# Turning eight tiles back by transposes before the first FFN, with theta begun in the last head

## The chip, the cores and the metric

One core of a Trainium2 chip. The metric is device time in microseconds: 641.4 us, the median of three runs of the kernel before (641.22 to 642.78).

## The reference, cut to what matters

x and ctx are (8, 256, 512), float32.

```python
x = x + tanh(g_xattn[0]) * L0_xattn(ctx, ctx, layernorm(x), ssm_kernel, D, 8)   # 32 heads of 8 channels: causal convolution
x = x + tanh(g_ffn[0])   * L0_ffn(layernorm(x), w1, b1, w2, b2)                 # int8 linear, exact gelu, int8 linear
x = x + tanh(g_xattn[1]) * L1_xattn(layernorm(x), ctx, theta_w, theta_b, ...)   # theta = theta_w @ ctx + theta_b, softmax, ...
x = x + tanh(g_ffn[1])   * L1_ffn(x, ...)                                       # 1.58-bit FFN
```

Both linears of the first FFN quantise their input with one scale for the whole tensor, so no product of the FFN can begin before the largest absolute value of all of layernorm(x) is known. theta needs ctx and weights alone.

## The kernel before, in words

The 2048 rows of x are 16 tiles of 128 x 512, taken in the order `order1` (even tiles first; numbers n below are places in it) in four groups of G = 4. Everything is ordered by hand: each engine has one instruction stream, and streams meet at semaphores `S[...]`.

**Heads.** In L0's attention each of the 32 heads runs through all engines: ScalarE repeats channels (`repeat_q` L830, `repeat_c` L809), GpSimd forms the pairs (`pairs` L612), TensorE multiplies by the Toeplitz matrix (`head` L1190, 20 passes of 128x288, banks 0 to 3 or 4 to 7 in turn), VectorE multiplies by q and sums (`head` L1622, the last instruction is L1638), GpSimd adds halves (`add_halves` L622) into `qT`. For the last head VectorE itself does the halves (L1693, L1695; semaphore `o_done`). Banks of PSUM have free columns beyond 288, in which other transposes travel with a head.

**Beside the heads.** Heads 20 to 27 turn back the tiles n = 0 to 7 by four transposes each (L1204), and VectorE adds them, read backwards and times tanh(g), to x (`back_add`, L1666). ScalarE turns the weights of the last FFN into ternary values (`ternary` L869, L873), whose loads and stores are SyncE's; in the loop of ScalarE, iteration h does `repeat_q(h + 1)`, `repeat_c(h + 2)`, then two `ternary` (in h = 28 the numbers 20 and 21, in h = 29 22 and 23). VectorE widens w1 from int16 to bf16 (`w1_widen` L1614) after heads 28 to 30, GpSimd the last quarter (L655).

**From head 31 to the first FFN.** TensorE adds x itself by a product with the identity (L1264) for six tiles, then turns tiles n = 8 to 15 back by products with `gated`, a reversed identity times tanh(g) (L1276). ScalarE copies six of them out of PSUM (L920), VectorE adds two (L1704). VectorE takes the maxima (`largest` L1677, L1679) and the statistics (L1557, L1561), GpSimd the scales (`norm_scales` L583), ScalarE normalises (L770). Then the maximum over all (transposed by TensorE, L1293), the scale `isx` (L1720), ScalarE's quantisation (`quant_x`, L945, two of them with `theta_out` between), VectorE's widening (`xqb_ready`, L1746), and TensorE's first linear (`mm1` L1308, L1313) with ScalarE's gelus (L952). The weights of theta and b1 are transposed after head 31 (L1260, L1262) and copied out by ScalarE (L926) and VectorE (L1697); eight `theta(b)` (L1286, four passes each, on the context loaded early by SyncE, L421 and L423) stand between those products, and `theta_out` (L932) takes each out.

**The store of x.** Group 0 of the hidden layer overwrites x, so x goes to HBM: GpSimd adds b2 to ten tiles after `xqb_ready` 3 (L661 to L663) and to six more (L666), SyncE stores each group when it is ready (`x1_save` L433, L437), and ScalarE's third group of gelus waits for all four (L969). In SyncE's queue the DMA transposes of the quantised tiles (L446) stand between these stores.

```python
            pool.wait_ge(S["xqb_ready"], 3)                                    # L661
            for t in order1[:10]:
                pool.tensor_tensor(x_res[:, t, :], x_res[:, t, :], b2b[:, :], ALU.add).then_inc(S["xb_added"], 1)

            gelu(1, 3, range(FT))
            act.wait_ge(S["x1_saved"], 16 * NG)                                # L969
            gelu(2, 0, range(FT))
```

## Time and profile before

| | |
|---|---|
| median of the runs | 641.4 us |
| the profiled execution | 643.1 us |
| its span | 641.3 us |
| mean granted clock of TensorE | 0.997 |
| busy: TensorE, VectorE, ScalarE, GpSimd | 95%, 85%, 74%, 55% of the span |
| chain that ended last | TensorE 65%, VectorE 12%, ScalarE 7% |
| the heads end (last head's product) | 196.4 us from the span's start |
| first product of the first FFN | 221.9 us |
| last product of its first linear | 283.4 us |

The profile is of one execution. A shares' table says which engine is worked hardest; what a change in one stretch is worth is read from the chain of waits in that stretch. Times in the rows are from the span's start.

### The profile page before, as it was taken

Reading aid. Unit: us, or ns where it says so; the run is one execution under the profiler, and the core shown is the slowest. Engines: PE = TensorE matmul, PEld = TensorE weight load, DVE = VectorE, ACT = ScalarE, POOL = GpSimd, SP = SyncE. Lnnn points to the kernel's source line nnn. Section 1 sums busy time; section 2 is a strip of 40 time slices with the busy share of each in tenths; the row PEclk is TensorE's granted clock in tenths of the full one; section 3 lists DMA queues with packets and bytes.
Section 4 is the critical chain, followed back from the end, with each engine's and each line's share of the span. In section 5 each row is a group of like instructions: output and inputs, shape, how many; then the busy total and the mean of one; then the engine's idle time right before and its main releaser. Section 6 shows DMA issues by size and latency. Waiting matters only on the chain.

```text
span 641.3 us, 9316 instructions
## 1 busy us (share of the span) xinstructions
PE 609.0 (95%) x2769; PEld 358.2 (56%) x2798; DVE 546.6 (85%) x1066; ACT 473.8 (74%) x718; POOL 351.9 (55%) x430
## 2 busy tenths in 40 slices
PE   5899999999999998989999999999888999999997
PEld 5777777777776443444445556555433444444443
DVE  2697888889999789976779988889898999999964
ACT  4469785765655896888672477766689999999984
POOL 1579888888874292310001111114487989898861
PEclk9999999999999999899999999999999999999999
DMA  8959896799999389838549920000116666656651
GB/s 300 377 192 310 291 327 223 260 323 339 332 299 331 134 285 311 223 94 327 198 98 167 255 56 16 16 17 17 50 33 162 185 177 183 164 180 164 182 162 50
DMA packets 141973, 125.20 MB, mean 195 GB/s; under 512 B 96032, under 2 KB 103984, under 8 KB 140784
## 3 DMA queue, kind: packets, MB, share of 16 engines
q1 hardware_dynamic: 134496, 110.52, 56.8%
q10 hardware_dynamic: 7440, 14.24, 6.6%
...
## 4 chain that ended last, share of the span: by engine, by line
PE 65%; DVE 12%; ACT 7%; issue 6%; DMA 4%; POOL 3%; SPq 2%; ACTq 0%; POOLq 0%; DVEq 0%
PE ps L1195 22%; PE ps L1475 14%; PE ps L1491 8%; PE ps L1313 4%; PE ps L1402 3%; PE ps L1432 3%; PE ps L1344 3%; DMA arena<-in_x 2%; ACT turn L989 2%; POOL arena L663 2%; PE ps L1450 2%; PE ps L1406 2%; SPq L446 2%; PE ps L1204 2%; DMA x_d<-arena 1%
## 5 line engine op out<-in xcount | busy, mean ns | idle before, releaser
L1195 PE MATMUL ps<-arena 128*128 128x288 f32 x640 | 160.6, 407 | 1.6 <-DVE inv_s L1661 0.9
L1195 PEld LDWEIGHTS ps<-arena 128*128 128x128 f32 x640 | 119.4, 190 | 33.5 <-DVE inv_s L1661 0.9
L1475 PE MATMUL ps<-arena 128*128 128x512 bf16 x510 | 113.5, 379 | 4.5 <-DVE arena L2066 4.3
L1475 PEld LDWEIGHTS ps<-arena 128*128 128x128 bf16 x512 | 49.4, 98 | 66.9 <-DVE arena L2066 5.7
L721 POOL TENSOR_TENSOR arena<-arena 128x512 f32<-128x512 f32 x64 | 80.4, 1276 | 8.6 <-DVE arena L2066 7.7
L618 POOL TENSOR_TENSOR arena<-arena 128x1024 f32<-128x1024 f32 x32 | 60.6, 1894 | 19.9 <-issue 12.3
L1313 PE MATMUL ps<-arena 128*128 128x512 bf16 (+1 forms) x249 | 57.1, 387 | 3.7 <-ACT arena L952 3.2
L1491 PE MATMUL ps<-arena 128*128 128x512 bf16 x241 | 57.1, 379 | 1.9 <-ACT arena L1103 0.7
L1344 PE MATMUL ps<-arena 128*128 128x512 bf16 x251 | 55.3, 379 | 1.2 <-DVE arena L1815 0.9
L952 ACT ACTIVATE arena<-ps,b,s 128x512 f32<-128x512 f32 x64 | 48.5, 778 | 10.6 <-DMA x_d<-arena 5.3
L625 POOL TENSOR_TENSOR turn<-turn 128x512 f32<-128x512 f32 x31 | 40.5, 1307 | 20.8 <-DVE turn L1638 20.8
L2066 DVE SCALAR_TENSOR_TENSOR arena<-ps,up_scale,arena 128x512 f32<-128x512 f32 x64 | 46.7, 745 | 5.8 <-ACT arena L1079 4.8
L579 POOL TENSOR_TENSOR ve<-mv,eps_ln 128x2 f32<-128x2 f32 x8 | 1.6, 198 | 87.5 <-DVE mv L1850 87.5
L1628 DVE TENSOR_TENSOR turn<-ps,arena 128x768 f32<-128x768 f32 x32 | 30.6, 955 | 18.3 <-PE ps L1204 15.5
L1313 PEld LDWEIGHTS ps<-arena 128*128 128x128 bf16 x256 | 25.3, 99 | 35.3 <-ACT arena L952 4.3
L1079 ACT ACTIVATE arena<-ps,up_scale 128x512 f32<-128x512 f32 x64 | 42.1, 675 | 3.9 <-PE ps L1475 3.8
L2073 DVE TENSOR_REDUCE q<-arena 128x1 f32<-128x1024 f32 x32 | 38.7, 1213 | 4.2 <-POOL arena L721 4.2
L1344 PEld LDWEIGHTS ps<-arena 128*128 128x128 bf16 x256 | 25.0, 98 | 30.8 <-issue 1.1
L1491 PEld LDWEIGHTS ps<-arena 128*128 128x128 bf16 x256 | 24.7, 98 | 30.7 <-ACT arena L1103 0.8
L715 POOL TENSOR_TENSOR arena<-turn,arena 128x1024 f32<-128x1024 f32 x16 | 37.8, 2363 | 5.5 <-ACT turn L1074 5.2
L1638 DVE TENSOR_TENSOR turn<-ps,turn 128x1024 f32<-128x1024 f32 x32 | 39.2, 1225 | 1.1
L873 ACT ACTIVATE late<-arena,inv_s 128x1024 int16<-128x1024 f32 x24 | 27.1, 1142 | 17.1 <-DMA arena<-in_L_ffn_w 15.5
...
## 6 DMA issues: line engine op xcount, KB each, us to landing
...
arena<-in_ctx SPq DMA_DIRECT2D x2, 2048.0 KB, 10.3
```

Of the source, the lines that this page charges most:

```text
L618: pool.tensor_tensor(dst[:, :, 0:32].rearrange("p r (d i) -> p r d i", d=4), a, shifted, ALU.mult)
L625: po.done(pool.tensor_tensor(x[:, :, 0:16], x[:, :, 0:16], x[:, :, 16:32], ALU.add))
L721: pool.tensor_tensor(hg[:, s, sl], hh[:, s, sl], g3[:, sl], ALU.mult).then_inc(S["hg_done"], 1)
L952: act.activation(hid[:, q, f, :], ps[:, f % 4, :], ACT.Gelu, bias=b1[:, f:f + 1], scale=s1[:, f:f + 1]).then_inc(S["gelu_done"], 1)
L1079: act.activation(sil[:, c, :], ps[:, up_banks(t, c)[0], :], ACT.Silu, scale=up_scale[:, s, 0:1]).then_inc(S["sil_done"], 1)
L1195: last = pe.matmul(ps[:, 4 * s + lo, 0:NB * PAIRS], toep[:, u, (LB - 1 - lo + li) * P:(LB - lo + li) * P], kv[:, s, li, :], start=(li == 0 ...
L1313: last = pe.matmul(ps[:, f % 4, :], fw1T[:, k, f * P:(f + 1) * P], xqT[:, k, ds(L * r, L)], start=(k == 0), stop=(k == LB - 1))
L1344: return pe.matmul(ps[:, 2 * j + f // 8, :], hq[:, r % 2, f, j * P:(j + 1) * P], fw2T[:, f, :], start=(f == first), stop=(f % 8 == 7))
L1475: last = pe.matmul(ps[:, bank, :], xq4T[:, s, 4 * j + k, :], w[:, k, c * L:(c + 1) * L], start=(k == 0), stop=(k == LB - 1))
L1491: last = pe.matmul(ps[:, 7 if s == 0 else 2, :], hqT[:, s, f, :], bw3T[:, f, :], start=(f == 0), stop=(f == FT - 1))
L1638: v.tensor_tensor(half[u], y[:, :, :, 0:32], pd, ALU.add).then_inc(S["prod_done"], 1)
L2066: v.scalar_tensor_tensor(out=hh[:, s % 2, c * L:(c + 1) * L], in0=ps[:, up_banks(t, c)[1], :], scalar=up_scale[:, s, 1:2], in1=sil[:, c, : ...
```

## The change

- `gated` becomes room for four tiles in `turn`. Tiles n = 8 to 15 are turned by four transposes each into banks 4 to 7; the identity products and the products with the reversed identity are gone.
- n = 8, 9, 12, 13 are added by VectorE straight from PSUM, read backwards, times tanh(g). n = 10, 11, 14, 15 are copied out by ScalarE with the scale, read backwards, and added by GpSimd.
- theta's weights and b1 are transposed with head 28, copied out by ScalarE in its iteration h = 29, and TensorE waits for these copies before head 30. theta 0 and 1 run after head 31, 2 to 7 after the turns.
- The context's first half is loaded by two DMAs from ScalarE in h = 29, the second by two from SyncE after the last head; before, each half was one DMA of SyncE.
- w1's quarters are widened two by ScalarE, two by GpSimd; VectorE takes the first maxima in the last heads instead. Its order after the last head is written out anew.
- GpSimd's `norm_x1(1)` comes before the halves of head 30. Two `theta_out` stand between the two quantisations.

```diff
-        dve_adds = [NT - 4, NT - 2]
-        act_copies = [n for n in range(NT // 2, NT) if n not in dve_adds]
+        dve_adds = [n for n in range(NT // 2, NT) if n % G < 2]
+        pool_adds = [n for n in range(NT // 2, NT) if n % G >= 2]
+        gated = turn[:, 0:4 * L].rearrange("p (m l) -> p m l", m=4)
 
...
             else:
-                eng.wait_ge(S["x1_out"], act_copies.index(n) + 1)
+                eng.wait_ge(S["x1_pool"], pool_adds.index(n) + 1)
+
+        def turned_back(n):
+
+            y = ps[:, 4 + n % G, :].rearrange("p (l c) -> p l c", l=LB)
+            return bass.AP(y.tensor, y.offset + P - 1, [list(y.ap[0]), [P, LB], [-1, P]])
...
-            sp.wait_ge(S["cd_ready"], HEADS)
-            sp.dma_start(ctx_early[0], ctx_rows[:, 0:NT // 2, :]).then_inc(c_in[1], 16)
             sp.wait_ge(S["prod_done"], HEADS + 2)
-            sp.dma_start(ctx_early[1], ctx_rows[:, NT // 2:NT, :]).then_inc(c_in[2], 16)
+            for part, c in ((0, 2), (1, 0)):
+                sp.dma_start(ctx_early[1][:, G * part:G * part + G, :],
+                             ctx_rows[:, NT // 2 + G * part:NT // 2 + G * part + G, :]).then_inc(c_in[c], 16)
...
-                if h == NT // 2:
-                    pool.wait_ge(S["tanh_done"], 1)
-                    pool.tensor_tensor(gated, bass.AP(identf[:, :].tensor, identf[:, :].offset + P - 1, [list(identf[:, :].ap[0]), [-1, P]]), tg[:, 0:1].to_broadcast([P, P]), ALU.mult).then_inc(S["gated_made"], 1)
...
-            for h in range(HEADS - 3, HEADS - 1):
-                add_halves(h, h % 2)
+            add_halves(HEADS - 3, 1)
             norm_x1(1)
-            pool.wait_ge(S["o_done"], HEADS + 2)
-            pool.wait_ge(S["w1_in"], 16 * 4)
-            w = fw1T[:, :, 3 * L:4 * L]
-            pool.tensor_scalar(w, w.bitcast(I16), 1.0, 0.0, ALU.mult, ALU.add).then_inc(S["w1_ready"], 1)
+            add_halves(HEADS - 2, 0)
+            for c in (2, 3):
+                w = fw1T[:, :, c * L:(c + 1) * L]
+                pool.wait_ge(S["w1_in"], 16 * c + 16)
+                pool.tensor_scalar(w, w.bitcast(I16), 1.0, 0.0, ALU.mult, ALU.add).then_inc(S["w1_ready"], 1)
+            for m, n in enumerate(pool_adds):
+                t = order1[n]
+                pool.wait_ge(S["x1_out"], m + 1)
+                pool.tensor_tensor(x_res[:, t, :], gated[:, m, :], x_res[:, t, :], ALU.add).then_inc(S["x1_pool"], 1)
...
+            def w1_widen(c):
+                w = fw1T[:, :, c * L:(c + 1) * L]
+                act.wait_ge(S["w1_in"], 16 * c + 16)
+                act.activation(w, w.bitcast(I16), ACT.Copy).then_inc(S["w1_ready"], 1)
...
+                if h == HEADS - 3:
+                    repeat_c(h + 2, h % 2)
+                    act.wait_ge(S["cd_ready"], HEADS)
+                    for part, c in ((0, 1), (1, 3)):
+                        act.dma_start(ctx_early[0][:, G * part:G * part + G, :],
+                                      ctx_rows[:, G * part:G * part + G, :]).then_inc(c_in[c], 16)
                 repeat_q(h + 1, 1 - h % 2)
                 if h + 2 == HEADS // 2:
                     act.wait_ge(S["c_out"], NT)
-                if h + 1 != HEADS // 2:
+                if h + 1 != HEADS // 2 and h != HEADS - 3:
                     repeat_c(h + 2, h % 2)
+                if h == HEADS - 3:
+                    act.wait_ge(S["prod_done"], HEADS - 4 + 3)
+                    act.activation(b1[:, :], ps[:, 0, NB * PAIRS:NB * PAIRS + FT], ACT.Copy).then_inc(S["b1_out"], 1)
+                    act.activation(th_w, ps[:, 1:3, NB * PAIRS:NB * PAIRS + P], ACT.Copy).then_inc(S["th_made"], 1)
+                    w1_widen(0)
...
                 for k in values_of(h):
+                    if k == TC - 1:
+                        repeat_q(HEADS - 1, 1)
                     ternary(k)
                 for n in w1_at(W1_QUANT, h):
...
+            def gated_copy(m):
+                act.wait_ge(S["back_tr"], pool_adds[m] + 1 - NT // 2)
+                act.activation(gated[:, m, :].rearrange("p (l c) -> p l c", l=LB), turned_back(pool_adds[m]), ACT.Copy,
+                               scale=tg[:, 0:1]).then_inc(S["x1_out"], 1)
+
+            def theta_out(b):
+                act.wait_ge(S["th_tr"], b + 1)
+                act.activation(th_made[b], ps[:, b % 4, :], ACT.Identity, bias=cols3[:, 0:1]).then_inc(S["th_made"], 1)
+
+            w1_widen(1)
...
-            act.wait_ge(S["small_in"], 96)
-            act.wait_ge(S["th_tr"], 1)
-            act.activation(th_w.rearrange("p d k -> p (d k)"), ps[:, 6, 0:2 * P], ACT.Copy).then_inc(S["th_made"], 1)
+            theta_out(0)
             act.activation(b2b[:, :], b2b[:, :], ACT.Copy, scale=tg[:, 2:3]).then_inc(S["b2_ready"], 1)
-            for n in act_copies:
-                x1_copy(n)
...
-            for n in range(2 * G, 3 * G):
+            theta_out(1)
+            for m in range(len(pool_adds)):
+                gated_copy(m)
+            theta_out(2)
+            theta_out(3)
+            for n in range(2 * G, NT):
                 normalise_x1(n)
-            theta_out(0)
-            theta_out(1)
-            for n in range(3 * G, NT):
-                normalise_x1(n)
-            theta_out(2)
+            theta_out(4)
+            theta_out(5)
...
-            for b in range(3, G + 2):
-                theta_out(b)
+            theta_out(6)
+            theta_out(7)
             quant_x(1)
-            for b in range(G + 2, NB):
-                theta_out(b)
...
+            def small_T(s):
+
+                pe.wait_ge(S["small_in"], 96)
+                pe.transpose(ps[:, 4 * s, NB * PAIRS:NB * PAIRS + FT], b1n, identf[0:FT, 0:FT])
+                for d in range(2):
+                    last = pe.transpose(ps[:, 4 * s + 1 + d, NB * PAIRS:NB * PAIRS + P], th_raw[:, d, :], identf[:, :])
+                return last
...
+                if h == HEADS - 4:
+                    last = small_T(s)
                 last.then_inc(S["y_ready"], 1)
...
+                if u == 2:
+                    pe.wait_ge(S["b1_out"], 1)
+                    pe.wait_ge(S["th_made"], 1)
                 head(HEADS - 4 + u, u % 2, None)
...
-            pe.wait_ge(S["prod_done"], HEADS + 1)
-            for n in act_copies:
-                if n == act_copies[G]:
-                    pe.wait_ge(S["prod_done"], HEADS + 2)
-                    pe.wait_ge(S["small_in"], 96)
-                    pe.transpose(ps[:, 4, 0:FT], b1n, identf[0:FT, 0:FT])
-                    for d in range(2):
-                        last = pe.transpose(ps[:, 6, d * P:(d + 1) * P], th_raw[:, d, :], identf[:, :])
-                    last.then_inc(S["th_tr"], 1)
-                pe.matmul(ps[:, n % 8, :], identf[:, :], x_res[:, order1[n], :], start=True, stop=False)
...
-            for n in range(NT // 2, NT):
-                b = order1[n] // 2
-                added = n in act_copies
...
-                for l in range(LB):
-                    src = qT[:, l * NB + b, P:2 * P]
-                    last = pe.matmul(ps[:, n % 8, l * P:(l + 1) * P], src, gated, start=not added, stop=not added or l == LB - 1)
...
-                if b % G == 0:
-                    pe.wait_ge(c_in[1 + b // G], 32)
-                if b == 0:
-                    pe.wait_ge(S["x1_out"], G)
+                if b % 2 == 0:
+                    pe.wait_ge(c_in[(1, 3, 2, 0)[b // 2]], 32)
...
+            def turn_back(n):
+                b = order1[n] // 2
+                if n >= NT // 2 + G:
+                    if n - G in dve_adds:
+                        pe.wait_ge(S["x1_dve"], 2 + NT // 2 + dve_adds.index(n - G) + 1)
+                    else:
+                        pe.wait_ge(S["x1_out"], pool_adds.index(n - G) + 1)
+                for l in range(LB):
+                    last = pe.transpose(ps[:, 4 + n % G, l * P:(l + 1) * P], qT[:, l * NB + b, P:2 * P], identf[:, :])
+                last.then_inc(S["back_tr"], 1)
+
+            pe.wait_ge(S["prod_done"], HEADS + 1)
+            theta(0)
+            theta(1)
+            pe.wait_ge(S["prod_done"], HEADS + 2)
+            pe.wait_ge(S["o_done"], HEADS + 2)
+            for n in range(NT // 2, NT):
+                turn_back(n)
+            for b in range(2, NB):
                 theta(b)
+            pe.wait_ge(S["x1_out"], len(pool_adds))
+            pe.wait_ge(S["x1_dve"], 2 + NT // 2 + len(dve_adds))
...
-            theta(G + 2)
-            theta(G + 3)
...
             def x1_add(n):
-                t = order1[n]
+                x = x_res[:, order1[n], :].rearrange("p (l c) -> p l c", l=LB)
                 v.wait_ge(S["back_tr"], n + 1 - NT // 2)
-                v.tensor_tensor(x_res[:, t, :], ps[:, n % 8, :], x_res[:, t, :], ALU.add).then_inc(S["x1_dve"], 1)
-
-            for g in range(2, NG):
-                for n in dve_adds if g == NG - 1 else ():
-                    x1_add(n)
-                stats([x_res[:, order1[G * g + j], :] for j in range(G)], g, S["st1"], S["rs1"],
-                      lambda j: x1_made(v, G * g + j))
-            for n in range(NT // 2, NT):
+                v.scalar_tensor_tensor(x, turned_back(n), tg[:, 0:1], x, ALU.mult, ALU.add).then_inc(S["x1_dve"], 1)
+
+            def x1_stats(n):
+                g, j = n // G, n % G
+                if j == 0:
+                    v.wait_ge(S["rs1"], g - 1)
+                x1_made(v, n)
+                dv.done(v.bn_stats(bn2[:, g % 2, j, :], x_res[:, order1[n], :]))
+
+            def x1_moments(g):
+                dv.wait()
+                for j in range(G):
+                    v.bn_aggr(mv2[:, g % 2, j, :], bn2[:, g % 2, j, :]).then_inc(S["st1"], 1)
+
+            largest(3)
+            x1_add(8)
+            largest(4)
+            x1_add(9)
+            x1_stats(8)
+            x1_stats(9)
+            x1_add(12)
+            x1_stats(10)
+            x1_add(13)
+            x1_stats(11)
+            x1_moments(2)
...
             for n in range(12, 16):
+                x1_stats(n)
+            x1_moments(3)
+            for n in range(5, NT):
                 largest(n)
```

## Rows read from the trace of the kernel before

**Rows 1.** The chain of waits from 165 to 235: start, length, what, in us.
```profile
177.74 14.83 PE ps L1195 x60
...
197.13 0.43 DVE arena L1695
...
213.94 0.70 DVE amax L1679
...
217.11 1.73 ACT arena L932 x3
...
221.62 12.82 POOL arena L663 x8
```

**Rows 2.** The chain of waits from 220 to 292.
```profile
246.86 9.62 DMA x_d<-arena
...
256.50 0.79 ACT arena L952
```

**Rows 3.** TensorE's timeline: start, us, line, operands, count.
```profile
172.02 0.60 PE L1204 MATMUL ps<-identf,arena 128*128 128x128 f32 x4
...
198.58 7.31 PE L1276 MATMUL ps<-sw2b,arena 128*128 128x128 f32 x64
205.73 8.75 PE L1286 MATMUL ps<-arena 128*128 128x512 f32 x20
```

**Rows 4.** ScalarE's timeline from 180 to 240, with the idle time before.
```profile
182.34 1.15 ACT L873 ACTIVATE late<-arena,inv_s 128x1024 int16<-128x1024 f32 x1 [0.76 <-DMA arena<-in_L_ffn_w]
183.39 0.61 ACT L832 ACTIVATE arena<-arena 128x512 f32<-128x512 f32 x1
183.91 0.40 ACT L812 ACTIVATE arena<-arena 128x256 f32<-128x256 f32 x1
184.22 0.29 ACT L813 ACTIVATE arena<-arena 128x128 f32<-128x128 f32 x1
...
198.62 0.36 ACT L926 ACTIVATE arena<-ps 128x256 f32<-128x256 f32 x1
...
207.01 2.93 ACT L770 ACTIVATE arena<-arena,shift,rstd 128x512 f32<-128x512 f32 x4 [0.49 <-POOL shift L597]
```

**Rows 5.** ScalarE's timeline at 114: two DMA issues on its queue.
```profile
114.23 0.38 ACTq L858 DMA_DIRECT2D arena<-in_L_ffn_w  x1
114.65 0.48 ACTq L797 DMA_DIRECT2D arena<-kpad_d  x1
```

**Rows 6.** VectorE's timeline, from 150 on.
```profile
176.95 0.73 DVE L1666 SCALAR_TENSOR_TENSOR arena<-ps,tg,arena 128x512 f32<-128x512 f32 x1
...
197.56 4.83 DVE L1679 TENSOR_REDUCE amax<-arena 128x1 f32<-128x512 f32 x8
202.30 2.46 DVE L1557 BATCH_NORM_STATS2 bn<-arena 128x6 f32<-128x512 f32 x4
204.80 0.38 DVE L1561 BATCH_NORM_AGGREGATE mv<-bn 128x2 f32<-128x6 f32 x4
```

**Rows 7.** The instructions of line L663 (GpSimd): minimum, median, maximum in ns.
```profile
L663 POOL TENSOR_TENSOR arena<-arena,b2b x10: 1260/1270/2258, 221.6 to 235.6; 128x512 f32<-128x512 f32 x10
```

**Rows 8.** ScalarE's groups by shape: count, busy us, mean ns.
```profile
L1098 ACT ACTIVATE arena<-arena 128x2048 bf16<-128x2048 int16 x15 | 28.5, 1897 | 0.0
```

**Rows 9.** Part 6 of the page: DMA issues, KB each, us to landing.
```profile
arena<-in_ctx SPq DMA_DIRECT2D x2, 2048.0 KB, 10.3
```

**Rows 10.** TensorE's timeline at its pause; then windows: busy by engine, granted clock, DMA.
```profile
257.33 26.03 PE L1313 MATMUL ps<-arena 128*128 x109 [3.23 <-ACT arena L952]
...
258.00:259.00 1.00, 1.00 (x4) 0.39 (x3) 1.00 (x2) 1.00 (x2) 0.00 (x0) 0.54 0.91 342
259.00:260.00 1.00, 1.00 (x3) 0.29 (x2) 1.00 (x1) 0.96 (x2) 0.00 (x0) 0.50 1.27 185
260.00:261.00 1.00, 1.00 (x4) 0.42 (x3) 1.00 (x2) 0.74 (x1) 0.00 (x0) 0.50 1.27 290
261.00:262.00 1.00, 1.00 (x5) 0.36 (x4) 1.00 (x1) 0.22 (x2) 0.04 (x1) 0.75 0.82 182
```

**Rows 11.** Line L1180 from 12 to 13 us: minimum, median, maximum in ns.
```profile
L1180 PE MATMUL ps<-identf,arena x10: 272/273/421, 11.6 to 13.0; 128*128 128x128 f32 x10
```

36 lines of the change are left out of this document (5 added, 31 removed).

## The prediction

> **What bounds the kernel now.** I read the chain of waits first, stretch by stretch, because every engine here is busy for long and only the chain says whose lateness moves the end. The reader should follow one line of work. [rows 1] TensorE runs heads 29, 30 and 31 without a gap, 14.83 us from 177.74, so 4.94 us a head and 182.68 as the start of head 30. VectorE ends the last half addition at 197.56, and this is `o_done`. The last maximum of tensor `amax` ends at 214.64. ScalarE then has three `theta_out` between its two quantisations, and GpSimd begins to add b2 at 221.62. [rows 2] goes on from there: GpSimd's additions release the stores of x1, the last of these lands at 256.48, and ScalarE starts the third group of gelus at 256.50; TensorE has by then stood still for 3.23 us. So inside the first FFN it isn't the matmuls that set the time but the store of x1, and that chain begins at 221.62. **The quantity to forecast is the start of those additions.** What comes sooner or later there passes on in full: SyncE's queue waits for GpSimd's eighth addition, and everything behind it hangs on it. TensorE's own gain before 254 goes into its pause.
>
> **Parts that cost nothing or little.** [rows 3] The identity products of six tiles and the 64 passes with `gated` (7.31 us) go; a head's four late transposes show what replaces the latter, 0.60 us in view and 0.48 to the start of the next matmul (172.50), so some 0.44 each, 8 x 0.44 = 3.5 us. But TensorE didn't end last here: the tile needed first was ready 0.9 us after `o_done`, and VectorE was then busy with `largest`. A theta is 8.75 / 5 = 1.75 us; thetas 0 and 1 move into the wait between head 31 and `o_done`, which hides them, and 2 to 7 take 10.5 us before the transpose of the maximum. They fit: from about 204.8 (below) to 215.3. GpSimd's `gated` product goes at h = 16, off the path. `small_T` adds three transposes to head 28, about 0.3 us to its end and 0.15 to head 29; I count it with the next term.
>
> **The new wait, the largest term.** The diff makes TensorE wait before head 30 for ScalarE's copies of b1 and theta's weights, and ScalarE makes them in the iteration h = 29, behind its other work there. [rows 4] In the run of before, ScalarE's last ternary of h = 28 waits for its weights until 182.34, and the queue is free for h = 29 at 183.39. From there, with the shapes of the same rows: `repeat_c` 0.31 to the next start and 0.29 for its second copy, 0.60, so 183.99; then the wait for its own `cd_ready` and two DMA issues on the same queue. [rows 5] Issues of ScalarE start 0.42 apart and take 0.38 and 0.48, so 0.85 for both, 184.85. `repeat_q` follows (0.52 from start to next start), the 16 columns of b1 (about 0.1), and the copy of 256 columns, 0.36 as `th_w` took before: 185.85. Head 30 then starts at about 185.9 instead of 182.68. **Heads 30 and 31 and `o_done` come 3.2 us later:** VectorE was tied to TensorE there (head 31's product began 0.03 us after its matmuls), `o_done` = 200.8. Queued behind the wait on TensorE are heads 30 and 31, both thetas and all turns; waiting for those is VectorE's product of head 30. The bounds of the wait: if both copies came right after head 28's product (181.7) it would be nothing; if the two issues took no time it would be 2.35 us; a ternary load that lands 1 us later makes it 4.2. I take the row, 3.2.
>
> **VectorE from `o_done` to the last maximum.** [rows 6] Pitches: a `largest` 0.59 (4.83 us for eight), a statistic 0.60, four moments 0.38 in view, a reversed addition out of PSUM 0.67 (its own predecessor, `back_add`: 0.73 in view). Before: 214.64 - 197.56 = 17.1 us, in which the chain was not VectorE's all the time. After, in the new order: 2 largest, 4 additions, 8 statistics, 2 x moments with their waits 0.43, and 11 largest: 1.2 + 2.7 + 4.8 + 0.9 + 6.5 = 16.0 us. No wait of it should hold: tile 8 is turned 0.5 us after `o_done`, the third tile at 202.25, ScalarE's first scaled copy (0.6) at 202.85. [rows 7] GpSimd adds in 1.27 us, so its tiles are ready at 204.2, 205.4, 206.7 and 208.0, against VectorE's need at 205.2, 206.5, 208.6 and 209.2. GpSimd's additions of tiles 14 and 15 stand ahead of `norm_x1(2)`, so the scales come at 208.0 + 1.8 = 209.8, and ScalarE's eight normalisations of 0.71 end at 215.5; plus a maximum 216.1, less than VectorE's own 216.85. So VectorE binds, 216.85 against 214.64: **3.2 - 1.05 = 2.2 us later.**
>
> **ScalarE after that.** Three `theta_out` between the quantisations become two: -0.57 ([rows 1], 1.73 / 3). The start of b2's additions: 221.62 + 3.2 - 1.05 - 0.57 = 223.2, **+1.6 us**. ScalarE's other new work is w1's widening, twice. [rows 8] The same shape and types take it 1.90 us elsewhere; the first lies in TensorE's head 30, the second in head 31 and the wait for `o_done`. The last ternary is the risk: the context's first half (2 MB) is now issued at 184.0, ahead of its load. [rows 9] Such a transfer took 10.3 us to land; wholly behind it the load comes at 195.2. Behind the ternary stand the widening, four normalisations, b2 and two `theta_out`: 1.05 + 1.9 + 2.85 + 1.75 = 7.6 us, so the first scaled copy would be at 202.8 instead of 202.25. VectorE has 1.0 us of room there. It costs nothing, because the stall has made room; without the stall it would cost up to 2.6 us.
>
> **TensorE's clock.** [rows 10] The one fall in this profile comes after the pause of 3.23 us: the granted clock is 1.00 when matmuls resume at 257.33, and from 258 to 262 it reads 0.54, 0.50, 0.50 and 0.75, so 1.2 GHz; 0.46 + 0.50 + 0.50 + 0.25 = 1.7 us of work lost. The new pause before head 30 is 185.9 - 182.85 = 3.05 us, hardly shorter, and heads 30 and 31 are on the path. I give it a little better than even that the clock falls there too, at 1.0 to 1.7 us, say 1.5. The pause in the FFN grows from 3.2 to about 5 us (TensorE arrives 0.4 sooner, x1 lands 1.6 later); its fall is paid already, and a different phase can move it by 1 us either way, in the range.
> Whether transposes keep the clock up matters as well, since there are now 3.5 us of them after a pause of 1.5. [rows 11] In the kernel's first transposes, with no other matmul before them, one still takes 421 ns at 12 us and those after it 272: transposes alone have raised it. The Trainium skill, TensorE: Matmul & The Clock Gate, Part 4 (PE-mode transpose), says that they don't count as busy and full clock doesn't engage; the trace disagrees.
>
> **Rivals.**
> *A: the wait alone, the clock stays up.* +1.6 us, 643.0. For it: the pause is a little shorter than the one that cost the clock.
> *B: the wait and the clock's fall before head 30 (forecast).* 1.6 + 1.5 = +3.1 us, 644.5. Both heads' ends and all after them move.
> *C: the other side, faster: the copies aren't late.* If `th_w` is copied by 182.85, TensorE doesn't pause, `o_done` stays at 197.56, and 1.05 + 0.57 = 1.6 us are gained, 639.8. It needs ScalarE 3 us earlier than [rows 4]; only an earlier load of the weights gives some of this, and then the ternary itself is still 1.05 us. A late last ternary would eat that gain.
> *D: the turned tiles lose the clock.* Thetas 2 and 3 would run at 1.2 GHz, `theta_out` 3 ends at 210.6 instead of 209.1 and holds ScalarE's normalisations 0.9 us; VectorE's room is 0.7, so +0.2 on A or B, and 1 us more if the fall lasts into the transpose of the maximum. This is what that page's rule would bring.
> *E: the change doesn't do what it says (a cheaper turn) on the path.* The turn was hidden in most of its length either way; contained in A and B.
>
> **How the numbers follow.** The profiled execution took 643.1 us with a span of 641.3, the median of the runs is 641.4; the sum is one of differences within the profiled run, 221.62 to 223.2 (A) or 224.7 (B), and I put it on the median. Chances: B 0.43, A 0.32, C or part of it (a shorter wait, below 641.9) 0.12, D or a longer wait (above 646) 0.13. B is likeliest: 641.4 + 3.1 = 644.5. The range reaches from A with a wait shorter by 1 us (642.0, rounded down to 641.8) to B with a load later by 1 us and a worse phase in the FFN, 646.4. A measurement of this kernel can tell about 0.3%, 1.9 us: faster than 639.5 needs all of C and more, 0.07; slower than 643.3 takes B, D, the longer wait and the upper end of A, 0.60; between 0.33.
>
> **What would show it.** After: an idle of about 3 us of TensorE before head 30 with a ScalarE copy as its releaser; ScalarE's two DMA issues at about 184; the granted clock at half in the following 3 us (B) or not (A); `o_done` at 200.8 or 202.3; VectorE without waits until the last maximum, 16 us later; b2's additions 1.6 or 3.1 us later than 221.6. Wrong if head 30 follows head 29 at once, if GpSimd's additions make VectorE wait for its statistics, or if the FFN's pause ends no later than before though b2's additions start later.

## The result, and the profile after it

The kernel after takes 646.66 us in the median of its runs, where the kernel before took 642.48 on the same chips: the ratio is 1.0063, with a 95% interval from 1.0048 to 1.0078, so 4.0 us slower (3.1 to 5.0). One run of 918.91 us was disturbed and is left out. The undisturbed runs of the kernel after spread from 642.89 to 648.22 us, and on the whole the longer ones have the lower mean granted clock (0.994 at 642.89, 0.992 at 643.22, 0.989 at 648.22 and 0.987 at 647.97). Its profiled run is that longest one, with a span of 646.4 us (before: 641.3), so its trace shows about 1 us more loss than the medians do.

The forecast was 644.5, 2.2 us below the measured median. Half of this is the base: three runs gave 641.4 for the kernel before and sixteen give 642.48. On the newer base the forecast of +3.1 us would be 645.6, and +3.1 is the lower end of the measured interval. The stated range ended 5.0 us above its own base (646.4), the measured median lies 4.2 us above its base (646.66).

The wait before head 30 came where it was forecast. ScalarE's timeline of the kernel after answers to [rows 4]; the columns are start, length, engine and line, operation, tiles, and in brackets the idle time before and what ended it:

```profile
182.63 1.15 ACT L879 ACTIVATE late<-arena,inv_s 128x1024 int16<-128x1024 f32 x1 [0.69 <-DMA arena<-in_L_ffn_w]
183.68 0.40 ACT L818 ACTIVATE arena<-arena 128x256 f32<-128x256 f32 x1
184.31 0.98 ACTq L903 DMA_DIRECT2D arena<-in_ctx  x2
185.33 0.63 ACT L838 ACTIVATE arena<-arena 128x512 f32<-128x512 f32 x1 [1.05 <-issue]
185.93 0.38 ACT L913 ACTIVATE arena<-ps 128x256 f32<-128x256 f32 x1
```

And TensorE's timeline of the kernel after, which answers to the first of [rows 1] and to [rows 3]:

```profile
186.52 11.34 PE L1224 MATMUL ps<-arena 128*128 128x288 f32 x40 [3.55 <-ACT b L912]
203.97 2.37 PE L1306 MATMUL ps<-identf,arena 128*128 128x128 f32 x20 [2.68 <-DVE arena L1713]
208.06 10.46 PE L1294 MATMUL ps<-arena 128*128 128x512 f32 x24
220.38 0.29 PE L1321 MATMUL ps<-identf,am 128*128 128x128 f32 x1 [1.85 <-DVE am L1749]
222.69 1.18 PE L1330 MATMUL ps<-identb,turn 128*128 128x128 bf16 x16 [2.02 <-DVE turn L1767]
224.89 6.28 PE L1338 MATMUL ps<-arena 128*128 128x512 bf16 x16 [1.02 <-DVE arena L1775]
```

Head 30 starts at 186.52 instead of 182.68, released by a copy of ScalarE, and heads 30 and 31 take 11.34 us instead of 2 x 4.94. The granted clock tells why (windows of 1 us; the third number from the end is the granted clock):

```profile
186.00:187.00 1.00, 0.48 (x1) 0.50 (x2) 1.00 (x1) 1.00 (x3) 0.66 (x2) 0.50 0.59 178
189.00:190.00 1.00, 1.00 (x5) 0.78 (x4) 0.00 (x0) 0.66 (x2) 0.92 (x4) 0.82 1.07 418
```

The two windows between read 0.50 too: 1.2 GHz for 3 us. Two things in this trace stood in no step of the sum. The first is on VectorE. The larger of its two half additions for the last head, 0.69 us in before (L1693), takes 1.67, and GpSimd's two widenings lie beside it (VectorE's timeline, then GpSimd's):

```profile
201.71 1.67 DVE L1711 TENSOR_TENSOR turn<-turn 128x512 f32<-128x512 f32 x1
203.41 0.42 DVE L1713 TENSOR_TENSOR arena<-turn 128x256 f32<-128x256 f32 x1
```
```profile
199.07 3.77 POOL L657 TENSOR_SCALAR arena<-arena 128x2048 bf16<-128x2048 int16 x2
226.51 3.71 POOL L669 TENSOR_TENSOR arena<-arena,b2b 128x512 f32<-128x512 f32 x3 [11.18 <-DVE turn L1781]
```

The second is a fall of the clock at 223 to 231 us. Before, thetas lay between the transpose of the maximum and the first FFN products; now TensorE idles 1.85, 2.02 and 1.02 us there, and the first 16 products take 6.28 us, at 0.50, where the same shape takes 3.6 at full clock. The windows of 1 us at its start and its end:

```profile
224.00:225.00 1.00, 0.11 (x1) 0.14 (x2) 0.63 (x2) 1.00 (x1) 0.00 (x0) 0.50 1.00 375
230.00:231.00 1.00, 1.00 (x5) 0.41 (x4) 0.00 (x0) 0.78 (x1) 1.00 (x2) 0.84 0.07 16
```

A third fall, at 291 to 296, lies at the start of the second FFN product. The one fall of the kernel before, at 258 to 262, is gone: the last 112 products of the first linear take 24.35 us, where before's took 26.03 (109 of them are on record, [rows 10]).

The ends that matter: `o_done` 203.8 (before 197.6), the last maximum 220.03 (214.64), b2's additions 226.51 (221.62, [rows 1]), and the gelu that waits for the store of x1 (as in [rows 2]) at 260.99 instead of 256.50:

```profile
260.99 1.45 ACT L975 ACTIVATE arena<-ps,b,s 128x512 f32<-128x512 f32 x2 [3.94 <-DMA x_d<-arena]
```

The gelu waits, but the store is not what set the end. The chain of waits of the kernel after (start, length, what) goes from the slow products and the second transposes of quantised rows into VectorE, and from 232.10 VectorE works without a wait until its last maximum of the hidden layer at 289.94; the store of x1 isn't in it:

```profile
224.89 6.28 PE ps L1338 x16
231.17 0.91 PE ps L1330 x16
232.10 1.23 DVE arena L1775
272.18 15.35 DVE hmax L1794 x7
290.66 0.16 DVE sx L1753
```

### The profile page after: what moved, and what is told of

Same layout as the page of the kernel before. It is cut to its first block, busy times and chain, and to the rows that moved or that the text cites. A ratio compares the mean times of both kernels' runs of the same rounds, so it can differ in the third digit from the quotient of the medians.

```text
span 646.4 us, 9261 instructions
## 1 busy us (share of the span) xinstructions
PE 605.8 (94%) x2754; PEld 353.9 (55%) x2754; DVE 547.7 (85%) x1064; ACT 477.3 (74%) x719; POOL 356.2 (55%) x434
## 4 chain that ended last, share of the span: by engine, by line
PE 51%; DVE 24%; DMA 7%; ACT 7%; issue 5%; SPq 3%; POOL 1%; ACTq 0%; DVEq 0%; POOLq 0%
PE ps L1498 14%; PE ps L1224 12%; PE ps L1514 8%; DVE hmax L1794 5%; DMA arena<-in_L_ffn_w 4%; PE ps L1425 3%; PE ps L1455 3%; DMA arena<-in_x 2%; ACT turn L1010 2%; PE ps L1367 2%; PE ps L1473 2%; PE ps L1429 2%; SPq L404 2%; PE ps L1405 1%; PE ps L1415 1%
## 5 line engine op out<-in xcount | busy, mean ns | idle before, releaser
L1498 PE MATMUL ps<-arena 128*128 128x512 bf16 x512 | 113.7, 379 | 4.0 <-DVE arena L2101 4.0
L1338 PE MATMUL ps<-arena 128*128 128x512 bf16 (+1 forms) x256 | 58.6, 392 | 3.0 <-ACT arena L975 2.0
L1367 PE MATMUL ps<-arena 128*128 128x512 bf16 x256 | 57.1, 386 | 2.6 <-DVE arena L1850 2.6
L1514 PE MATMUL ps<-arena 128*128 128x512 bf16 x256 | 58.2, 379 | 1.0 <-ACT arena L1124 0.7
```

Of the source, the lines that this page charges most:

```text
L1338: last = pe.matmul(ps[:, f % 4, :], fw1T[:, k, f * P:(f + 1) * P], xqT[:, k, ds(L * r, L)], start=(k == 0), stop=(k == LB - 1))
L1367: return pe.matmul(ps[:, 2 * j + f // 8, :], hq[:, r % 2, f, j * P:(j + 1) * P], fw2T[:, f, :], start=(f == first), stop=(f % 8 == 7))
L1498: last = pe.matmul(ps[:, bank, :], xq4T[:, s, 4 * j + k, :], w[:, k, c * L:(c + 1) * L], start=(k == 0), stop=(k == LB - 1))
L1514: last = pe.matmul(ps[:, 7 if s == 0 else 2, :], hqT[:, s, f, :], bw3T[:, f, :], start=(f == 0), stop=(f == FT - 1))
```

## The experiments

Each was timed in five rounds beside the kernel before on its own chip. Edits are against the kernel after, if nothing else is said. "Fillings" are transposes or products of the identity into an unused part of PSUM, in idle time of TensorE; they don't change what is computed.

**One table for all.** From each kernel's profiled run, in us: start of head 30 (182.7, rounded, where the heads run through), end of VectorE's half additions (`o_done`), start of b2's additions, the gelu released by x1's store (a dash where none waits), and VectorE's scale of the second FFN quantisation ("scale 2", the tile sx); then the span, the median of the runs, and the ratio to before with its interval.

| kernel | head 30 | o_done | b2 | x1 | scale 2 | span | median | ratio |
|---|---|---|---|---|---|---|---|---|
| before | 182.68 | 197.6 | 221.62 | 256.50 | 286.18 | 641.3 | 642.48 | |
| after | 186.52 | 203.8 | 226.51 | 260.99 | 290.66 | 646.4 | 646.66 | 1.0063 (1.0048-1.0078) |
| e1 | 182.7 | 198.3 | 220.95 | 254.15 | 284.26 | 640.4 | 643.00 | 1.0007 (0.9991-1.0023) |
| e2 | 185.24 | 201.1 | 224.10 | 258.04 | 287.71 | 642.5 | 645.80 | 1.0064 (1.0040-1.0088) |
| e3 | 185.35 | 202.8 | 225.46 | 260.01 | 289.38 | 644.2 | 645.98 | 1.0065 (1.0036-1.0094) |
| e4 | 185.08 | 201.7 | 225.13 | 259.76 | 289.86 | 646.0 | 646.58 | 1.0065 (1.0044-1.0085) |
| e5 | 182.7 | 198.7 | 222.09 | 256.67 | 287.26 | 642.0 | 643.09 | 1.0009 (0.9995-1.0022) |
| e6 | 183.85 | 199.8 | 222.43 | 257.08 | 285.36 | 640.1 | 644.65 | 1.0039 (1.0020-1.0057) |
| e7 | 186.08 | 202.5 | 226.58 | 261.10 | 289.43 | 644.2 | 646.05 | 1.0059 (1.0037-1.0082) |
| e8 | 185.64 | 201.5 | 224.74 | 260.71 | 291.16 | 645.9 | 647.46 | 1.0083 (1.0059-1.0107) |
| e9 | 182.7 | 198.4 | 221.71 | - | 285.67 | 642.0 | 643.54 | 1.0008 (0.9998-1.0018) |
| e10 | 185.57 | 201.5 | 224.78 | - | 287.91 | 643.8 | 645.69 | 1.0047 (1.0029-1.0064) |
| e11 | 182.7 | 197.7 | 221.76 | - | 285.90 | 642.7 | 643.96 | 1.0016 (1.0005-1.0027) |
| e12 | 182.7 | 197.9 | 220.50 | - | 284.62 | 641.6 | 643.50 | 1.0010 (0.9997-1.0023) |
| e13 | 182.7 | 198.0 | 222.55 | - | 286.76 | 641.7 | 642.26 | 0.9995 (0.9984-1.0005) |
| e14 | 185.15 | 201.1 | 224.45 | 257.80 | 288.48 | 643.2 | 646.73 | 1.0070 (1.0054-1.0085) |
| e15 | 182.7 | 197.4 | 221.44 | - | 285.29 | 640.1 | 642.33 | 1.0002 (0.9993-1.0012) |
| e16 | 185.41 | 200.3 | 223.79 | 258.77 | 289.00 | 643.8 | 646.31 | 1.0063 (1.0041-1.0085) |

A trace is one execution and can lie 1.3 to 1.7 us beside its kernel's median (after, e2, e4, e13, e14), that of e6 2.7 us below it, the fastest of its eight runs. After and the experiments were timed in five groups, each with its own runs of the kernel before (medians 642.48 to 642.82), so verdicts on the time go by the ratios, and the traces say where it went.

**The wait, taken out and put in: e1 and e7.**

```diff
 # e1: in ScalarE's head 28, ahead of its last ternary tile
+if k == TC - 3:
+    act.wait_ge(S["prod_done"], HEADS - 4 + 3)
+    act.activation(b1[:, :], ps[...], ACT.Copy).then_inc(S["b1_out"], 1)
+    act.activation(th_w, ps[...], ACT.Copy).then_inc(S["th_made"], 1)
 ...
 # (and not in head 29)
```

> The changed kernel, with ScalarE's copies of b1 and theta's weights moved ahead of ternary 21 (iteration h = 28), so that they are done when TensorE ends head 29. Theory W (the wait before head 30 costs 3.8 us and 1.6 us more through the clock): TensorE has no pause before head 30, granted clock 1.00 there, the last half addition (o_done) at about 198.5 instead of 203.8 in the span, and the time falls by 3 to 5 us against the changed kernel, so about equal to the kernel before. Rival X (the pause only takes time from a later wait, the last ternary's load at 193.4): o_done is earlier, but ScalarE reaches the scaled copies so late that the maximum over all comes less than 2 us sooner, and the time falls by less than 2 us.

```diff
 # e7, against the kernel BEFORE: ScalarE, head 29, and TensorE, head 30
+for n in range(5):
+    act.wait_ge(S["held"], n)
+    act.activation(spare[:, :], b2b[:, 0:P], ACT.Copy).then_inc(S["held"], 1)
 ...
+if u == 2: pe.wait_ge(S["held"], 5)
```

> The kernel before with only the wait added: in head 29 ScalarE makes five copies of 128x128 into an unused tile, each waiting for the one before, and TensorE's head 30 waits for the last; nothing else of the change is in it. It should hold head 30 by 2.5 to 4 us (start 185.2 to 186.7 instead of 182.68). The theory that the wait is the whole cost of the change: the time rises by as much plus up to 1.5 us for the clock, 645.1 to 648 against 642.6. The rival, that the wait costs only with the missing thetas between the quantisations (no work on TensorE there, second fall of the clock): here the thetas are in place, so the rise is the wait and its own fall alone, and the trace shows the clock at 1.00 from 213 to 230. If the store of x1 doesn't bind, the rise is 1.5 us or more less than the wait.

TensorE's timeline of e1: the three heads run through, as in [rows 1], at a granted clock of 1.00 throughout.

```profile
177.61 14.72 PE L1225 MATMUL ps<-arena 128*128 128x288 f32 x60
193.98 3.67 PE L1295 MATMUL ps<-arena 128*128 128x512 f32 x8 [1.66 <-DMA arena<-in_ctx]
219.80 5.79 PE L1339 MATMUL ps<-arena 128*128 128x512 bf16 x16 [0.99 <-DVE arena L1776]
```

TensorE's timeline of e7: the kernel before with a pause of 2.96 us, a fall of the clock behind it (x40 in 11.44 us), and no fall before the FFN (16 products in 3.62).

```profile
186.08 11.44 PE L1200 MATMUL ps<-arena 128*128 128x288 f32 x40 [2.96 <-issue]
226.66 3.62 PE L1320 MATMUL ps<-arena 128*128 128x512 bf16 x16
261.93 24.35 PE L1320 MATMUL ps<-arena 128*128 x112 [2.92 <-ACT arena L957]
```

Without the wait the ratio falls from 1.0063 to 1.0007, 3.6 us; with the wait alone the kernel before rises to 1.0059, 3.8 us. The intervals are about 1 to 1.5 us wide on either side. The two agree from both sides: **the wait with what it brings is all of the loss that can be measured**. The rest of the change, gains and losses together, comes to nothing that can be told. Rival C of the prediction, 1.6 us below the kernel before without the wait, is refuted: e1 is 0.4 us above it, and its interval reaches down to 0.6 us below. Its gain on VectorE and ScalarE is there, but b2's additions start only 0.7 us sooner than before's, since the slower half addition takes 1.0 us of it.

**How the wait is made up: e6 and e2.**

```diff
 # e6: ScalarE, head 29: the two DMA issues of the context behind the copies
-    (ahead of repeat_q)
+    (behind the copies of b1 and th_w)
     act.wait_ge(S["cd_ready"], HEADS)
     act.dma_start(ctx_early[0]..., ctx_rows...)   # twice
```

> The kernel after with ScalarE's two issues of the context's first half put behind the two copies (b1 and theta's weights) in head 29, nothing else changed. The wait theory: the two issues (0.98 us in the profile of after) leave the path to head 30, which starts about 1.0 us earlier (185.5 instead of 186.5, TensorE's pause 2.6 instead of 3.55). If the time follows the start of head 30: 645.6 against 646.7 for after. If the pause of 2.6 us still drops the clock, that 1.0 us is all; if it doesn't, another 1.5 us goes, 644.1. The rival, that the pause is covered by what follows: no change, 646.7.

```diff
 # e2: TensorE, ahead of head 30
+pe.wait_ge(S["prod_done"], HEADS - 4 + 3)
+for _ in range(27): pe.transpose(ps[:, 3, ...], identf[:, :], identf[:, :])
 pe.wait_ge(S["b1_out"], 1)
```

> The changed kernel, with 27 transposes of the identity on TensorE in the pause before head 30; nothing reads them. Theory: the clock's fall there is caused by the pause alone. The pause's end stays where it is (186.5), the granted clock stays 1.00 through heads 30 and 31, head 30 takes 4.9 us instead of 6.5, and o_done comes 1.6 us sooner. If transposes don't count as work for the clock (the rival, the rule of the Trainium skill, TensorE: Matmul & The Clock Gate, Part 4), it falls all the same. Time: 0.5 to 1.6 us below the changed kernel.

In the kernels with the wait the last ternary tile of head 28 and head 30 keep one distance: 182.63 and 186.52 in after, 181.47 and 185.35 in e3, 181.67 and 185.57 in e10, 181.24 and 185.15 in e14, so 3.9 us. When that tile starts is the landing of its load, and that moves from execution to execution: 179.76 (e2), 180.26 (e8), 181.1 to 181.7 in the others, 182.63 in after, the latest of nine. It moves in the kernel before too: 182.34 in before, 182.25 in e7, 181.73 in e15, and in e11 the tile starts at about 180.1 without a wait. In e6 the distance is 2.72 (ScalarE's timeline):

```profile
181.13 1.15 ACT L879 ACTIVATE late<-arena,inv_s 128x1024 int16<-128x1024 f32 x1 [1.01 <-DMA arena<-in_L_ffn_w]
182.69 0.61 ACT L838 ACTIVATE arena<-arena 128x512 f32<-128x512 f32 x1
182.82 0.40 ACTq L912 DMA_DIRECT2D arena<-in_ctx  x1
183.28 0.37 ACT L909 ACTIVATE arena<-ps 128x256 f32<-128x256 f32 x1
```

So the two issues are 1.2 us of the wait, and the ratio fell by 0.0024, 1.5 us, with intervals that overlap. In e2 the clock stays up over the pause filled with transposes (TensorE's timeline):

```profile
182.29 3.11 PE L1286 MATMUL ps<-identf 128*128 128x128 f32 x27
185.24 9.87 PE L1224 MATMUL ps<-arena 128*128 128x288 f32 x40
201.22 5.35 PE L1309 MATMUL ps<-identf,arena 128*128 128x128 f32 x32 [2.68 <-DVE arena L1716]
```

Heads 30 and 31 take 9.87 us, at 1.00, so the 1.5 us of after's fall is gone. That the transposes did this is not shown by e2 alone: with the early load the pause would have been only about 1.4 us without them, and e10, e14 and e16 held the clock over 2.3 to 2.5 us with no filling. The time didn't fall (1.0064), and the trace has two reasons. First, my count was fixed and the wait isn't: the load landed early, ScalarE's last copy ended at 183.63, and the transposes themselves held head 30 until 185.24, some 1.4 us. So e2 doesn't price the clock, and e8 has the same fault. Second, the clock fell behind the next idle time, the 2.68 us in which TensorE waits for `o_done`, and the turns take 5.35 us instead of 3.9. **With no fall in the heads it came in the turned tiles** in e8, e10 and e14 too, and in e9, which has no wait before head 30 (in e6 and e16 in neither). There it costs about 0.6 us: from `o_done` to b2's additions it is 22.7 us in after, e3 and e6 and 23.3 in e8, e9, e10 and e14.

**The idle time before the FFN: e3, e5 and e8.**

```diff
 # e3: TensorE around the transpose of the maximum (14, 14) and behind rows_T(0) (6)
+for _ in range(n): pe.transpose(ps[:, 6, 0:P], identf[:, :], identf[:, :])
 # e5: e3 and e1 together.  e8: e3 and e2 together.
```

> The changed kernel, with 14, 14 and 6 transposes of the identity on TensorE in the three gaps between theta 7 and the first product of the FFN (ahead of and behind the transpose of the maximum, and behind rows_T(0)); nothing reads them. Theory: the fall of the clock from 223.4 to 230.7 comes from these gaps, in which the kernel before had thetas. The clock stays 1.00, the first 16 products take 3.6 us instead of 6.3, rows_T(1) comes about 2.7 us sooner, and since VectorE's chain through the FFN hangs on it, the time falls by 1.5 to 2.7 us. Rival: the store of x1 binds from there as in the kernel before, and the time stays within 0.5 us.

> The kernel after with the two copies put ahead of the ternary tile, as in e1 (no wait before head 30), and with e3's 14, 14 and 6 idle-time transposes on TensorE before the first FFN. The three theories of what sets the time once the wait is gone. Clock theory (the fall of the clock at 217 to 225 us in e1 is what keeps it at the time of before): the clock stays at 1.00 from 215 to 250, VectorE's wait for the second set of turned rows falls from 3.15 to about 0.5 us, the time falls by 2 to 2.6 us, to about 640.5 against 642.6 for the kernel before. Store theory (the store of x1, landed at about 254.1 in e1, sets the time of the FFN): TensorE comes to it 2.2 us earlier, pauses 2.5 to 3.5 us there, the clock falls in that pause as it did in e3, and the time is that of e1, 642.5 to 643.2. Third, if neither holds (code or contention of the added transposes): over 643.5.

> The kernel after with both fillings: 27 transposes on TensorE in the pause before head 30 (e2) and 14, 14 and 6 before the first FFN (e3). It prices the clock with the wait left in. Clock theory: heads 30 and 31 at full clock, clock 1.00 at 217 to 250, the start of the quantised rows about 1.5 us earlier than in after (GpSimd's b2 additions at about 225 instead of 226.5), time 644 to 645 against 646.7 for after. Store and wait theory: since e2 and e3 gained 0.7 us at most each, the pause at the store of x1 grows to 4 us and eats what VectorE gained, time 645.3 to 646.5.

The fillings did their work: the 16 products take 3.61 us in all three, and VectorE's wait for the next turned rows falls from 3.2 to 0.5 us. The time didn't follow. TensorE came earlier to the gelu that waits for x1's store, stood longer, and the clock fell there instead. TensorE's timeline of e5:

```profile
220.48 3.61 PE L1344 MATMUL ps<-arena 128*128 128x512 bf16 x16 [0.48 <-DVE arena L1782]
257.50 4.88 PE L1344 MATMUL ps<-arena 128*128 x11 [3.80 <-ACT arena L976]
```

In e3, e5 and e8 the chain of waits goes through x1's store, as in before, and no longer through VectorE, as in after and e1. e5 is e1 to 0.1 us, as the store theory had it, and e3 has after's ratio (1.0065 and 1.0063). e8, where that theory said 645.3 to 646.5, came out above after (1.0083): its transposes held head 30 by some 1.3 us, as in e2 (the last copy ended at 184.06, head 30 began at 185.64), and x1's gelu came 36.0 us behind b2's start instead of the usual 33 to 35, for which I have no cause.

**Which of the two ends last: e9, e10, e11.**

```diff
 # SyncE's queue (e9 in e5, e10 in after, e11 in the kernel BEFORE)
-w2_store(0)
 x1_save(3)
+w2_store(0)
```

> The kernel e5 (copies early, idle-time transposes before the first FFN) with one more edit: on SyncE's queue the last quarter of x1's store goes ahead of the second FFN's first weight store and its load, instead of behind them. Store theory (the landing of x1 sets the FFN's end: in the nine profiles so far the second quantisation scale came 28.3 to 30.6 us after it): x1 lands 3 to 5 us earlier than in e5 (256.67), at 252 to 254, TensorE's pause of 3.8 us goes and its fall of the clock with it, the second scale comes at 284 to 285.5 (e5: 287.26), and the time is 640 to 641.5, below both kernels. Rival, that VectorE's chain of maxima and quantisations is what counts: in e5 it starts 2.5 us earlier than in e1 and isn't what waits, so the time falls to 641 or less as well only if the landing moves; if the time stays at 643 with the landing earlier, the store theory is wrong.

> The kernel after with only that exchange on SyncE's queue (x1's last quarter ahead of the second FFN's first weight store and load). Store theory alone: x1 lands 3 us earlier than 260.99, the time falls by 2 us or more, to 644.7 or less. Two-chains theory (in after VectorE's chain from the second set of turned rows to the second scale has no wait longer than 0.2 us, so it ends as late as the store's): the landing moves, TensorE's pause of 1.63 us goes, the second scale stays at 290 to 290.7 and the time within 0.6 us of after, 646.1 to 646.9, since only e3's filling moves VectorE's chain.

> The kernel before with only that exchange on SyncE's queue, as the control of e9 and e10. In before VectorE's chain from 226.25 us to the second scale is unbroken too, so by the two-chains theory at most 0.7 us is gained, 642 to 642.8 against 642.6, though TensorE's pause of 3.23 us and its fall go. By the store theory alone x1 lands 2 to 3 us before 256.5 and the time falls by as much, 640 to 640.6.

In all three the gelus no longer wait for x1, and nothing is gained beyond doubt: e9 has 1.0008, e11 1.0016 and so is slower than the kernel before by 1.0 us (0.3 to 1.7), and e10 is 1 us below after, with intervals that overlap. The forecasts for e9 (640 to 641.5) and e11 (642 to 642.8, or 640 by the store alone) failed, and e10's 645.69 lies between its two. VectorE's timeline of e9 shows what is late next, the second FFN's weight that the store was let past, and TensorE's shows the end of the product before and a wait of 6.30 us with the clock at half behind it:

```profile
256.12 2.29 DVE L1626 TENSOR_REDUCE sw<-late 128x1 f32<-128x2048 f32 x1 [2.52 <-DMA late<-in_L_ffn_w]
```
```profile
278.34 1.16 PE L1366 MATMUL ps<-sw2b,mean_w 128*128 128x128 f32 x8 [0.87 <-ACT arena L976]
287.02 5.73 PE L1374 MATMUL ps<-arena 128*128 128x512 bf16 x15 [6.30 <-DVE arena L1857]
```

So three chains end nearly together, and the eighteen traces sort by which of them the chain of waits runs through. It goes through x1's store in before, e2, e3, e5, e7 and e8; through VectorE's unbroken work behind the second turned rows in after, e1, e4, e6, e10, e14 and e16; and through the second FFN's weight in e9, e11, e12, e13 and e15. In before VectorE's chain is not unbroken, though the expectation for e11 said so: it waits 1.54 and 0.79 us for gelus behind the store. VectorE's timeline of before:

```profile
280.76 2.29 DVE L1759 TENSOR_REDUCE hmax<-arena 128x1 f32<-128x2048 f32 x1 [0.79 <-ACT arena L952]
```

So the store sets the time in before, by about 2.3 us over VectorE and hardly at all over the weight: with the store out of the way scale 2 comes at 285.90 in e11 instead of 286.18. In after it sets nothing.

**The contended addition, and the fall before the second FFN product: e4, e12 to e16.**

```diff
 # e4: GpSimd, ahead of the two widenings
+pool.wait_ge(S["o_done"], HEADS + 2)
 # e12: e9, with the two widenings ahead of add_halves(HEADS - 2, 0)
 # e13: e12; e14: after; e15: e11; e16: e4, each with more idle-time products on TensorE
-for n in range(22):
+for n in range(98):     # e13; 54 in e14 and e16, 92 in e15
     pe.matmul(ps[:, 2, ...], identb[:, :], identb[:, :], start=True, stop=True)
```

> The changed kernel, with GpSimd's two widenings of w1 held back until o_done. Theory: VectorE's first half addition takes 1.67 us instead of 0.69 because GpSimd widens int16 to bf16 at the same time; without that it takes 0.7 and o_done comes 1.0 us sooner. But GpSimd's widenings then end 3.8 us after o_done, so its first addition starts up to 1.3 us later than its tile is ready, VectorE waits for its statistics, and of the 1.0 us some 0 to 0.5 are left in the time. Rival: the slow addition has another cause, and it stays at 1.67.

> The kernel e9 with GpSimd's two widenings of w1 put ahead of head 30's half additions instead of behind them, so that they don't lie beside VectorE's last half addition of head 31. Contention theory (that addition took 0.69 us in before and in e4, 1.67 beside the widenings in after, 1.66 in e1): it takes 0.69 again, o_done comes about 1.0 us earlier, and the time falls by up to 1 us below e9's, 639.3 to 640.8. Rivals: w1's turned quarters have not landed at 190.7 us, or head 30's sums come later and the turning back waits for GpSimd: no gain or a loss against e9.

> The kernel e12 with 98 instead of 22 idle-time products on TensorE ahead of the second FFN product (4.8 us more of them, in an idle time of 6.46 us). Fall theory: in e12 the second scale came at 284.62 us, earlier than before's 286.18, but its span was 357.0 us longer than that, against 354.7 where the clock did not fall; filled, the clock stays at 1.00 from 280 to 298 and the time falls by 1.6 to 2.3 us, to 641.2 to 641.9 against 643.5 for e12 and 642.8 for before. Rival: the idle time before the product is VectorE's and the fall is hidden by what follows: 643.5.

> The kernel after with 54 instead of 22 idle-time products ahead of the second FFN product (2.0 us more, in an idle time of 2.58 us), nothing else changed. Fall theory: no half clock at 291 to 296 us, the time 1.0 us less than after's, 645.7 against 646.7. Rival: only the trace shows it, the time stays within 0.3 us.

> The kernel before with the exchange on SyncE's queue (e11) and 92 instead of 22 idle-time products ahead of the second FFN product (4.4 us more, in an idle time of 5.62 us). Fall theory: e11's 643.96 falls by 1.5 to 2.1 us, to 641.9 to 642.5, the second scale stays at 285.9. With e13 it tells what the change's own work is worth: if e13 is below e15 by 1 us or more, the turned tiles gain once the wait is gone; if they are within 0.5 us, they gain nothing.

> The kernel e4 (GpSimd's two widenings of w1 behind o_done) with 54 instead of 22 idle-time products ahead of the second FFN product (2.0 us more, in an idle time of 3.0 us). Contention theory: 0.5 to 1.0 us less than e14, since the scale comes 0.8 us earlier and no fall of the clock takes it back: 644.8 to 645.2. Rival: the slower half addition is hidden behind something else, and the time is that of e14, 645.7.

With the widenings moved, VectorE's addition is 0.69 us again (e4; VectorE's timeline), which shows the cause of the 1.67. But the widenings now hold up GpSimd's own additions, and VectorE waits for one of them:

```profile
200.55 0.69 DVE L1712 TENSOR_TENSOR turn<-turn 128x512 f32<-128x512 f32 x1
206.82 0.69 DVE L1726 BATCH_NORM_STATS2 bn<-arena 128x6 f32<-128x512 f32 x1 [0.47 <-POOL arena L662]
```

Its worth in time is less plain. In e4 and e16 it is 23.4 to 23.5 us from `o_done` to b2's additions instead of 22.7, so 0.8 of the 1.0 us is given back, and e4 has after's time and e16 is 0.4 us below e14, less than can be told. These two repairs are no fair test. e12's is a better one: nothing is given back there, though the addition takes 0.97 us (0.86 in e13) and not the 0.69 that I had expected. b2 starts 1.2 us sooner than in e9, about half of it because the turned tiles ran at full clock, and scale 2 comes 1.05 us sooner. Yet its time is e9's, 643.5, where I had expected 639.3 to 640.8. The fillings before the second FFN product show what ate part of it. TensorE's timeline of e12, then of e13:

```profile
285.98 5.85 PE L1374 MATMUL ps<-arena 128*128 128x512 bf16 x15 [6.46 <-DVE arena L1857]
```
```profile
280.16 5.63 PE L1369 MATMUL ps<-identb 128*128 128x128 bf16 x98
288.32 3.40 PE L1374 MATMUL ps<-arena 128*128 128x512 bf16 x15 [2.53 <-DVE arena L1857]
```

The 15 products take 3.40 us instead of 5.85. From scale 2 to the end of the span it is 354.7 to 355.1 us in each of the eleven traces whose clock held there and 355.7 to 357.0 in the seven whose clock fell. In time the filling is worth about 1 us by the ratios, from 1.0016 (e11) to 1.0002 (e15) and from 1.0010 (e12) to 0.9995 (e13), with intervals that overlap in both pairs. In e14 it brought nothing (646.73; expected 645.7), though its trace shows no fall there, and e16, at 646.31, missed its 644.8 to 645.2. e13, the change without its wait and its falls and with most of the contention gone, and e15, the kernel before with the same repairs, are equal within their intervals: 642.26 and 642.33. Neither can be told from the kernel before, so no version beats it.

## Why the prediction was right and wrong

**Right: the side, the place and the mechanism.** Slower, by the new wait before head 30. TensorE idles 3.55 us there (forecast: about 3) with a copy of ScalarE as releaser, the two DMA issues are at 184.3 (184), the clock is at half for the following 3 us (B), and e1 and e7 show that the wait is the loss.

**Right: VectorE from `o_done` to the last maximum.** 16.2 us for 16.0 forecast (203.8 to 220.03), without a wait of over 0.25 us. One `theta_out` less between the quantisations: from the last maximum to b2's additions 6.5 us instead of 7.0, so 0.5 for 0.57.

**Right: the late ternary load costs nothing.** It started at 193.45, 3.5 us later than before (forecast: up to 195.2 less its margin), and ScalarE still stood 3.49 us before the first scaled copy, so the stall had made the room. The other half of that sentence holds too: without the stall, where the load landed late, it did cost. In e13 the tile started at 194.80 instead of e12's 189.19, VectorE waited 1.65 us for one of GpSimd's additions, and b2's additions started 2.05 us later (forecast: up to 2.6).

**Wrong: the sum was too small, 3.1 for 4.0 us (4.2 between the medians).** At b2's additions the trace of after has +4.89 where the sum had +3.1. Its terms: the wait 3.84 for 3.2, the fall 1.47 (11.34 less e2's 9.87) for 1.5, the larger half addition +0.98 for nothing, VectorE's order -0.9 for -1.05, ScalarE -0.5 for -0.57; together 4.9. **The step that failed is the sum of the path from head 28 to `o_done`**, in two terms. (1) The wait: its chain on ScalarE was right (3.9 us behind the ternary tile), but it was 0.3 short from the two issues and the semaphores, and the load landed 0.3 later than before's in this execution. In the other eight with the wait it landed 0.6 to 2.6 earlier than before's, so the wait is 2.4 to 2.9 us in e3, e4, e10, e14 and e16, less than I said. (2) The half additions: I took L1693's 0.69 over because its code was unchanged, and the diff put two GpSimd widenings beside it. This term is in every trace of the kernel after and of its variants with the widenings in place (1.66 or 1.67), and is the mis-sized one. The prediction followed GpSimd's moved work for its own time and not for what it does to VectorE.

**Executions differ.** e10 and e14 are the kernel after up to 240 us, and b2's additions start at 224.78 and 224.45 there, +3.2 and +2.8, against +4.9 in the profiled run of after. Their wait was 2.9 and 2.5 us and no fall came in the heads, but the contention (1.67 both) and the turned tiles' fall did come. So an execution is neither my A nor my B: a wait of 2.4 to 3.8, contention 1.0, VectorE's and ScalarE's gain of 1.4, and a fall of 0.6 or 1.5 (B's). The 0.6 is in rival D's place and in its range of price, by another route: the turned tiles themselves ran at half clock, and the thetas behind them at full (24 passes in 10.47 us). That e10's +3.2 and e14's +2.8 lie so near the forecast's +3.1 is luck: a shorter wait and a cheaper fall stand against the contention that the sum left out.

**Wrong: "what bounds it now", for the kernel after.** I said that the store of x1 sets the time inside the FFN and that a shift of b2's start passes on in full. That reads the kernel before rightly, but the change moved the bound. In after the store isn't in the chain of waits; VectorE is, from 232.10 on. x1 at +4.49 and scale 2 at +4.48 look like a shift passed on and are a coincidence: VectorE starts on the second turned rows 5.85 us later than before (232.10 for 226.25), and 2.33 us of before's waits behind the store are gone. In e7, where the store does bind, b2's start moved by 4.96 and scale 2 by 3.25, 1.7 less. I had also called the fall of the clock in the FFN's pause "paid already". It can go away: the products behind the pause take 24.35 us instead of 26.03 in after and in e7, and 1.7 us is what e7 gets back. The pause's growth to 5 us failed too: in after it is 1.63, since TensorE itself was late by the second fall.

**Missed: the thetas between the quantisations.** I costed their move at nothing, since they fit. They also kept TensorE busy there, and without them the clock falls at 217 to 225 (e1) or 223 to 231 (after). In after this fall is in the chain of waits: it is why VectorE starts late on the turned rows. Filling the idle time (e3, e5) hands the chain back to the store, whose longer pause brings a fall of its own, and gains nothing measurable: a step that was wrong in the trace and, by luck, right in the time.

**Not settled.** The medians' 4.2 us is 1.0 to 1.4 more than e10's and e14's shifts of b2's start. (e14's trace is of the fastest of its six runs, 1.7 us below their median, so its shift is not the usual one; e10's is at its median.) A fall before the second FFN product would fit (0.6 to 2.3 us in the traces), but e14 removed it and its median stayed. So of the 1.1 us by which the forecast was short, the contention is seen in the traces, as 1.0 us at `o_done`, and is not shown in the time: e4 and e16 took it away, e12 most of it, and the medians fell by 0.1 (e4), 0.4 (e16) and 0.0 us (e12), with intervals of about 1 to 1.5 us on either side, e4 and e16 by a repair that gives back 0.8 us, and e12 where the second FFN's weight sets the time. A kernel after with the widenings ahead of head 30's halves and nothing else changed was not run.
